# Splitting the softmax normalisation of the large attention heads between VectorE and GpSimd, with a new order of all five engines

## The reference, cut to what matters

```
q, k, v = heads(ln @ Wq), heads(kv_input @ Wk), heads(kv_input @ Wv)    # kv_input = context (128) and latents (64)
sim = einsum('bhid,bhjd->bhij', q * scale, k)                            # 64 x 192 per sequence and head
sim = sim - max(sim, axis=-1)
attn = exp(sim) / sum(exp(sim), axis=-1)
out = einsum('bhij,bhjd->bhid', attn, v)
```

## Time and profile before

| | |
|---|---|
| median of 3 runs | 2493.83 us (2493.24 to 2495.58) |
| the profiled execution, its own time | 2495.97 us |
| its span in the trace | 2494.2 us |
| mean granted TensorE clock in the span | 0.988 |
| instructions | 41897 |
| busy: TensorE / VectorE / ScalarE / GpSimd | 2345.5 / 1481.6 / 1178.3 / 930.0 us |

### The profile page before, as it was taken

How to read it: one execution, slowest core, us unless ns; L and a number is a source line. 1 busy time by engine, 2 the same in 40 slices (tenths; PEclk the granted TensorE clock), 3 DMA queues, 4 the chain that set the end, 5 groups by cost and what they waited for, 6 DMA issues and landing times.

```text
span 2494.2 us, 41897 instructions
## 1 busy us (share of the span) xinstructions
PE 2345.5 (94%) x16412; PEld 1563.5 (63%) x16412; DVE 1481.6 (59%) x4040; ACT 1178.3 (47%) x2994; POOL 930.0 (37%) x853
## 2 busy tenths in 40 slices
PE   8999999999999999999999999999999999999998
PEld 5666665656756665666666665566566666656665
DVE  5457566665575667666564567665555555664653
ACT  4554334455444534545554444445454444354543
POOL 5334253533233335434231344443332242544310
PEclk8999999999999999999999999999999999999999
DMA  5000000000000000000000000000000000000000
GB/s 233 1 1 2 1 9 8 11 1 18 1 1 10 1 1 10 9 10 9 10 1 9 1 1 9 1 10 9 14 1 1 5 1 1 1 1 1 2 1 9
DMA packets 6677, 26.57 MB, mean 11 GB/s; under 512 B 848, under 2 KB 848, under 8 KB 5840
## 3 DMA queue, kind: packets, MB, share of 16 engines
q1 hardware_dynamic: 6480, 23.89, 2.6%
HBM read 21.79 MB, written 2.10 MB: 10 GB/s over the span
## 4 chain that ended last, share of the span: by engine, by line
PE 72%; DVE 17%; POOL 4%; ACT 4%; issue 3%; DMA 0%; SPq 0%; DVEq 0%; POOLq 0%; ACTq 0%
PE ps L472 10%; PE ps L485 7%; PE ps L529 6%; PE ps L504 6%; PE ps L868 4%; PE ps L496 3%; PE ps L608 3%; PE ps L457 3%; PE ps L583 3%; PE ps L576 3%; PE ps L630 3%; PE ps L581 2%; PE ps L825 2%; PE ps L815 2%; PE ps L657 2%
## 5 line engine op out<-in xcount | busy, mean ns | idle before, releaser
L1882 POOL TENSOR_TENSOR P<-P,small 128x384 f32<-128x384 f32 x384 | 317.2, 849 | 550.1 <-DVE small L1400 549.8
L1114 ACT ACTIVATE P<-ps,small 128x192 f32<-128x192 f32 x768 | 313.6, 420 | 155.1 <-DVE small L1392 153.5
L1855 POOL TENSOR_TENSOR small<-small,mhalf 128x4 f32<-128x4 f32 x112 | 129.0, 1152 | 547.2 <-DVE small L1380 315.4
L485 PE MATMUL ps<-kvT,big 128*128 128x192 f32 x1536 | 314.1, 335 | 6.7 <-DVE big L1407 2.5
L485 PEld LDWEIGHTS ps<-kvT,big 128*128 128x128 f32 x1536 | 248.6, 191 | 89.7 <-issue 52.8
L1392 DVE TENSOR_REDUCE small<-ps 128x2 f32<-128x384 f32 x384 | 210.1, 551 | 107.5 <-PE ps L485 100.2
L472 PEld LDWEIGHTS ps<-wts,P 128*128 128x128 f32 x1920 | 231.5, 192 | 43.8 <-issue 30.0
L472 PE MATMUL ps<-wts,P 128*128 128x128 f32 x1920 | 249.0, 279 | 5.2 <-POOL P L1972 2.6
L1972 POOL TENSOR_TENSOR P<-T 128x512 f32<-128x512 f32 x96 | 126.6, 1319 | 206.6 <-ACT T L1261 107.7
L504 PEld LDWEIGHTS ps<-value,big 128*128 128x128 f32 x1536 | 177.8, 192 | 25.8 <-issue 19.6
L504 PE MATMUL ps<-value,big 128*128 128x128 f32 x1536 | 188.0, 277 | 0.0
(11 more groups left out here) (281 smaller groups left out, 4476.8 us busy)
## 6 DMA issues: line engine op xcount, KB each, us to landing
ctok<-ctok_dram SPq DMA_DIRECT2D x8, 512.0 KB, 3.5
ctxT<-ctx_dram SPq DMA_DIRECT2D x8, 512.0 KB, 3.5
wts<-weights_dram SPq DMA_DIRECT2D x1, 2530.0 KB, 23.9
wts<-weights_dram SPq DMA_DIRECT2D x1, 2189.0 KB, 18.3
X<-x_dram SPq DMA_DIRECT2D x8, 256.0 KB, 3.0
big<-fold_dram SPq DMA_DIRECT2D x2, 1024.0 KB, 9.2
out_dram<-X SPq DMA_DIRECT2D x8, 256.0 KB, 2.0
wts<-weights_dram SPq DMA_DIRECT2D x1, 1536.0 KB, 27.0
```

The source lines that it names most:

```text
L485: m = pe.matmul(ps[s][:, at:at + KEYS], big[s][:, BANK * b + 128 * p:BANK * b + 128 * p + 128], kvT[s][:, keys_at(b):keys_at(b) + KEYS], s ...
L1114: m = act.activation(probs(s, b // 2)[:, to:to + KEYS], ps[s][:, at:at + KEYS], ACT.Exp, bias=small[s][:, 4 * e + p:4 * e + p + 1], accum_ ...
L1855: pool.tensor_tensor(rstd(s, name, n), variance(s, name, n), mhalf[:, 0:n], ALU.pow).then_inc(*sig("rstd", s))
L1882: m = pool.tensor_tensor(view, view, over(small[s][:, at:at + 2], 2, [128, 2, KEYS]), ALU.mult)
```

## The change

The second block of each pair is normalised by VectorE, half by half, each half as soon as its own exponentials are there. The first block stays with GpSimd, also by halves. Reciprocals are now taken by halves for both blocks. TensorE waits for each half of a block ahead of the two transposes that read it. `rsum` counts 6 for each pair now: the two reciprocals of the first block, and reciprocal and product of each half of the second. In the stage's program for VectorE the steps of the first block's halves come ahead of the reductions of the second block's halves. All numbers of `ORDER` but that of SyncE are new (the VectorE program has 2422 steps where it had 2038).

```diff
-    pe=(2496, int(""
-        "4120180e82000011000000000033dbffdf375f56bac10c1af4ddee629cc55cb06914148810afbdc018a1ca1dd3aea84c3e9c"
...
+    pe=(2496, int(""
+        "411000d600100020000000000093ffe3efb7eaebea0e182bf8d7c79820afa78981d28291409f5efa859439d7754824007b3f"
...
-                    def turn_p(j, k, at):
+                    def turn_p(j, k, at, half_ready=None):
                         for p in range(4):
+                            if half_ready and p % 2 == 0:
+                                pe.wait_ge(*half_ready(p // 2))
                             m = pe.transpose(part(s, k, p), probs(s, j)[:, PAIR * p + at:PAIR * p + at + 128], C("ident"))
...
-                        pe.wait_ge(*on("p_ready", s, i, u))
-                        turn_p(j, 2, 0)
+                        turn_p(j, 2, 0, lambda hf: on("p_ready", s, i, 2 * v + hf))
...
-                        pe.wait_ge(*on("p_ready", s, i, u + 1))
-                        turn_p(j, 3, CTX)
+                        if j == 0 and g != 1:
+                            pe.wait_ge(*on("exped", s, i, 2 * (u + 1) + 1))
+                        turn_p(j, 3, CTX, lambda hf: on("rsum", s, i, 6 * v + 3 + 2 * hf))
...
-                    def inverse(b):
-                        e = b % 2
-                        yield
-                        dve.wait_ge(*on("exped", s, i, 2 * (8 * g + b) + 1))
-                        dve.reciprocal(small[s][:, 16 + 4 * e:20 + 4 * e], small[s][:, 8 + 4 * e:12 + 4 * e]).then_inc(*sig("rsum", s))
+                    def normalise(b, hf):
+                        at = 4 * (b % 2) + 2 * hf
+                        inverse = 6 * (4 * g + b // 2) + (2 + 2 * hf if b % 2 else hf)
+                        yield
+                        dve.wait_ge(*on("exped", s, i, 2 * (8 * g + b) + hf))
+                        dve.reciprocal(small[s][:, 16 + at:18 + at], small[s][:, 8 + at:10 + at]).then_inc(*sig("rsum", s))
+                        if b % 2:
+                            yield
+                            dve.wait_ge(*on("rsum", s, i, inverse))
+                            view = p_seq(s, b, 2 * hf, 2 * hf + 2)
+                            dve.tensor_tensor(view, view, over(small[s][:, 16 + at:18 + at], 2, [128, 2, KEYS]), ALU.mult)\
+                                .then_inc(*sig("rsum", s))
...
                         if j < PAIRS - 1:
+                            yield from normalise(2 * j + 2, 0)
                             yield from negmax(2 * j + 3, 0)
-                            yield from inverse(2 * j + 2)
+                            yield from normalise(2 * j + 2, 1)
                             yield from negmax(2 * j + 3, 1)
-                            yield from inverse(2 * j + 3)
+                            yield from normalise(2 * j + 3, 0)
+                            yield from normalise(2 * j + 3, 1)
...
-                    def normalise(b):
-                        e = b % 2
-                        yield
-                        pool.wait_ge(*on("rsum", s, i, 8 * g + b))
+                    for j in range(PAIRS):
                         for hf in range(2):
-                            view, at = p_seq(s, b, 2 * hf, 2 * hf + 2), 16 + 4 * e + 2 * hf
-                            m = pool.tensor_tensor(view, view, over(small[s][:, at:at + 2], 2, [128, 2, KEYS]), ALU.mult)
-                        m.then_inc(*sig("p_ready", s))
...
+                            view, at = p_seq(s, 2 * j, 2 * hf, 2 * hf + 2), 16 + 2 * hf
+                            yield
+                            pool.wait_ge(*on("rsum", s, i, 6 * (4 * g + j) + hf))
+                            pool.tensor_tensor(view, view, over(small[s][:, at:at + 2], 2, [128, 2, KEYS]), ALU.mult)\
+                                .then_inc(*sig("p_ready", s))
```

More of the change, by code:

```diff
@@ new lines @@
+        "a73ed7fe170748270fffff", 16)),
+    act=(1740, int(""
+        "440024028020000000093ff9e7febd3efeeac6c203c1930f02411844166e77b42307b361586066e00f1e02fff5981ff8b677"
+        "9db12a17bdc02fd0022000c783387ffffbffdb9f7bea85604bc1930f02411800822a8eeef1373180606db1e073ba317fffef"
+        "e8103c0474ebf0a48dfb8ff00000004ef0ce7f7f7fc7df7fbeec5c143fee0cc02401c000822af78bf07dfb0c36181e4e018f"
+        "718bffff510b1bc03bdca51cc3d18fe800000056b8ce7eeffee7de88bd1652fe840ffd4c3c0a04c0224882f7fcbffeff1454"
+        "01dad73fffffcf5e7fdec477c9f901fff", 16)),
@@ new lines @@
+    dve=(2422, int(""
+        "180383828480000200000000001b7ffb7e787fb7b7917c8f8e2776fc9b7eb8c03f103ce2fdc96343777ce003a6063b9cc0b0"
+        "607070f138402389b89703dbef7f70dfffffdb372e603990ca1b832840bb8500620f200000000003bfffbbfbfffffa4de63c"
+        "7138ff69b7cc4633f403cf0fdc5668371c0706310364829cf30370f920803193c277e1cd8f77aff7fffff83dd500019139f7"
+        "1c0385435dc54000002002c101f00025bfffb7f5ef726c03f1fffd7aefeb7f1813fff8f227b15170b077401830d0364836ba"
+        "f00bfd1f043c203a07c14effe6efd6feafbf83fd840c3cce70397c001882dc542008014100003d0002abddff5fdbff23c03f"
+        "121cbe77e633fbe70385fffe787f6292d196073b0c83c240841cff73f5ffc3841990cb7fffffffffffffff3777400ecfffd", 16)),
@@ L135 @@
         "logits": LOGITS, "shifted": LOGITS[:3], "u_exp": LOGITS[:3], "n_proj": PROJ,
-        "qp_ps": 12, "qp_act": 12, "qp_dve": 12, "scores": 48, "maxed": 48, "exped": 48, "rsum": 24, "p_ready": 24,
+        "qp_ps": 12, "qp_act": 12, "qp_dve": 12, "scores": 48, "maxed": 48, "exped": 48, "rsum": 72, "p_ready": 24,
         "pT_ps": 36, "pT_act": 24, "pT_dve": 12, "mixed": 12, "mix_dve": 12, "mix_act": 12, "heads_ps": 3,
@@ L1412, in heads @@
                     yield from negmax(0, 1)
+                    yield from normalise(0, 0)
                     yield from negmax(1, 0)
-                    yield from inverse(0)
+                    yield from normalise(0, 1)
                     yield from negmax(1, 1)
-                    yield from inverse(1)
+                    yield from normalise(1, 0)
+                    yield from normalise(1, 1)
                     for j in range(PAIRS):
@@ L1875, in heads @@
                 def heads(s, i, g):
-                    def normalise(b):
-                        e = b % 2
-                        yield
-                        pool.wait_ge(*on("rsum", s, i, 8 * g + b))
+                    for j in range(PAIRS):
                         for hf in range(2):
-                            view, at = p_seq(s, b, 2 * hf, 2 * hf + 2), 16 + 4 * e + 2 * hf
-                            m = pool.tensor_tensor(view, view, over(small[s][:, at:at + 2], 2, [128, 2, KEYS]), ALU.mult)
-                        m.then_inc(*sig("p_ready", s))
-                    for b in range(GB):
-                        yield from normalise(b)
-                        if g == 0 and b == 3:
+                            view, at = p_seq(s, 2 * j, 2 * hf, 2 * hf + 2), 16 + 2 * hf
[3 more added lines that the diff above has]
+                                .then_inc(*sig("p_ready", s))
+                        if g == 0 and j == 1:
                             yield from preset_heads(s, i)
```

27 lines of the change are left out of this document (7 added, 20 removed).

## The result

The change makes the kernel slower by 61 us: 2555.44 us at the median of 4 runs (2553.40 to 2555.98), against 2494.70 of the kernel before (4 runs beside them). The ratio is 1.0236, with an interval from 1.0218 to 1.0253. The predicted 2488 us was wrong in its sign, and the result lies above the end of the range, 2514. The profiled execution took 2555.15 us, with a span of 2553.3 and a mean granted clock of 0.985 (0.988 before).

The account below looks back on a forecast made before the run. TensorE, busy 2345.5 of 2494.2 us, was taken as the bound. Terms -7 + 7 + 6 - 12 = -6 us gave 2490 against the profiled 2495.97, or 2488 us against the median 2493.83; range 2464 to 2514.

Parts of the forecast that it names:

- The order searched anew: New interleaving on four engines uses idle time ahead of the heads stage's matmuls: -12 us, bounds -24 and +12.
- The prediction's own test: If waits near the heads stage are as before but time differs by over 5 us, the order's term was wrong.
- VectorE's queue (+7): At 72 pair borders the next reduction stands 0.6 us longer behind a product: +7 us, bounds 0 and +43.
- load (+6): More VectorE work, 138 us (+4), and products held up by GpSimd (+2): +6 us, bounds 0 and +34.
- the meetings: New VectorE products held up by GpSimd operations: 192 x 0.317 = 61 us of VectorE, worth +2 on TensorE.
- How much reaches TensorE?: Scores waited for exponentials 59 times in 384 groups, so 15% of 43 us border delay reaches TensorE: +7 us.
- The gain (-7): Second block leaves GpSimd and is released 1.1 us earlier, shrinking TensorE's 9.2 us of waits: -7, bounds 0 and -9.
- A, slower by the queue: Products on VectorE's critical queue at pair borders; half the 43 us reaches TensorE: +21, 2515 us, chance 0.18.
- its two signs: ScalarE's wait for reductions grows from 153.5 us towards 190; the scores' wait for exponentials rises above 28.5.
- B, mutual exclusion: VectorE's new products and GpSimd's operations in heads stages exclude one another: +22, 2516 us, chance 0.10.
- Neither of its signs: The new product's mean is over 1 us; TensorE's waits for the norm's last product grow.

Follow-up runs that it names:

- old order: All five engines in the ORDER of the kernel before; the whole change put into it took 2531.40 us, ratio 1.0151.
- new order: The ORDER of the changed kernel, searched anew with the change; the whole change in it took 2555.44 us, ratio 1.0236.
- small, one input: Whole change, each second-block product on VectorE replaced by a maximum over 2 x 2 elements, one SBUF input: 2494.97 us in the old order, 2529.41 in the new order.
- small, two inputs: Whole change, second-block products on VectorE cut to 2 of 192 keys: 2506.80 us in the old order, 2547.28 us in the new order.
- full length, one input: Whole change, each second-block product on VectorE replaced by a maximum over the same 128 x 384 elements: 2517.40 us in the old order, 2541.85 in the new order.
- the runs with the copy first: Whole change, VectorE's mixed copy put ahead of the next second block's reciprocals and products: 2535.94 us in the old order, 2636.29 us in the new order.
- the halves on GpSimd: Kernel before, its order kept, all products on GpSimd, reciprocals and releases by halves: 2490.31 us (0.9975), in a second group 2491.84 us (0.9981).

## Why the prediction was wrong, point by point

The eight medians of the table (us) carry it. "The product itself" is the whole change:

```
                          old order   new order
small, one input            2495.0      2529.4
small, two inputs           2506.8      2547.3
full length, one input      2517.4      2541.9
the product itself          2531.4      2555.4
```

**The order searched anew: this is the step that failed.** The prediction took -12 us, with bounds of -24 and +12, "rests on no duration and is the weakest". It measured +34 in the row with the small maxima, and +24 in the row with the products. The upper bound was the weakest of all: it was the lower one turned round, from the idle time near the heads stages, while every stage on four engines was laid out anew. Without this term's error alone (-12 became +34) the forecast would have been 2534. The prediction's own test pointed the wrong way in part: the waits near the heads stage were not as before, and the order was still at fault.

**VectorE's queue (+7) and load (+6): 13 us taken, 36 measured in the old order and 26 in the new.** The places were right, but the share that reaches TensorE was not. In the old order the meetings cost 12 us by themselves and the length 22, together 34 of the 36; in the new order 18 and 12, which together are 4 more than the 26 of both. Taken at full length, as product against one input, the meetings cost 14 us in either order.

The step that failed for the length was "How much reaches TensorE?". It followed the next reduction, the exponentials and the scores, and took 15% from 59 waits. Of these 59 only 3, 1.4 us in all, were waits of the scores' matmuls; 56 were of the weight loads ahead of them. Along that path next to nothing came: in the old order the matmuls' wait for exponentials was 2.1 us with small maxima, 2.5 with full length and 3.0 with the products. The path that counted is the other one. The products of 72 borders stand ahead of the copy as well, on which the next transposes wait, and the transposes' wait put down to "issue" went with the time in the four kernels of the old order: 4.1, 8.4, 20.5 and 27.9 us at 2495.0, 2506.8, 2517.4 and 2531.4 us. That is 24 of the 36 us; since the runs with the copy first brought in a wait of their own, no run takes this path away alone.

For the meetings I took 61 us on VectorE and 2 us on TensorE. VectorE lost only 19 us: 23 of the 192 products of the changed kernel were held up by 0.2 us or more, the longest by 1.6 us. But these 19 us cost 12 to 18. The scaling of TensorE's waits by VectorE's load (9% more load, 9% more waiting) has no place for that; why so much of it arrives is not shown.

**The gain (-7): about -1 to -5.** The waits for the second block are gone and GpSimd's product stands in no wait of TensorE in the changed kernel, as predicted. In the time that shows little: -1 in the run with small maxima in the old order, whose interval reaches from -6 to 0 and in which VectorE still has 35 us more to do than before (1516.6 against 1481.6), and -5 or a little less with the halves on GpSimd, which took away 7.0 us of waits.

**The sum by measured terms:** -1 (relief and halves) + 34 (order) + 26 (products in that order) = +59 us against 60.7 measured; by the other way round the table it is -1 + 36 (products in the old order) + 24 (order with them). Both sums come out by construction, since each term is the step from one kernel to the next, and confirm nothing by themselves; the remaining 1.2 us is the difference between the medians of before in the two groups.

**The rivals.** A, slower by the queue, had the border right and the share of half nearly: of 43 us of delay, 12 to 22 arrived, the load included. It had the wrong thing behind the products. Of its two signs the first failed: ScalarE's wait for reductions is 151.5 us, not 190, while the transposes behind the copy lost 17.8 us instead of 5.7. The second came, the scores' wait for exponentials growing from 28.5 to 45.8 us in the view of the earlier trace rows, but it is the order's: the kernel with small maxima in the new order has 45.9 us there, and the whole change in the old order 34.1. B, mutual exclusion, is shown in its mechanism by the durations above. Neither of its signs came: the mean is 657 ns and not over 1 us, and TensorE's wait for the norm's last product fell from 33.0 to 23.5 us. Its price was 12 to 18 us, where +30 had been worked out. I had let each of these two rivals stand beside an order that wins or holds its ground, and none had the order itself lose.

The Trainium skill (SBUF — State Buffer, section "SBUF: two separate sides") says that a VectorE operation with two SBUF inputs and a GpSimd operation that reads SBUF exclude one another. By that rule the trace agrees: with two inputs even 4 elements took up to 1.77 us, and with one input 384 elements never took over 555 ns.

**What stays open.** Why the new order is worse on identical instructions is not settled. Its losses lie in many small waits, and what the search that made it went by can't be seen from here. Engines' orders were not exchanged one by one between the kernels, nor was the new order run with all products on GpSimd; neither was tried. By the medians the new order suits the products somewhat better than the old one (26 against 36 us), which the spread of the runs nearly covers; that it was made for other durations than the chip's is only a guess.

## What to carry to other kernels

An order searched anew for a tuned kernel is a change of its own, with a price that can be larger than the edit's; run the edit in the old order first, and cost the new order with a loss as large as any gain. Before work is moved onto an engine, list everything behind it in that engine's queue, not only the next user of the same data, and price a block of 2 us by what waits for it, not by its share of the engine's load. Putting the urgent instruction first is no cure by itself: where it has to wait, the whole queue waits with it. The better use of the same idea here was to leave the work on the idle engine and only start each half earlier.

## What the runs showed of the hardware

A VectorE product on 128 x 4 elements, both inputs in SBUF, took 164 ns at the median and up to 1767 ns (old order) or 1971 ns (new order). Those that were held up in the old order all overlapped an operation of GpSimd. A reduction of 128 x 384 elements with one input, from the same buffer, took 552 to 555 ns in all 192 cases of one kernel, and a product of 128 x 512 with one of its inputs in PSUM 690 to 693 ns in all 128 cases of the changed kernel. When both products of a pair met GpSimd's context operations, they took up VectorE for 4.3 us instead of the 1.1 of two medians. GpSimd's own operations took 1.99 and 2.19 us there, and 1.99 us where least disturbed, so that GpSimd, being first, gave 0.2 us where VectorE gave 3.
